# Attention and FFN block: four query projections move into attention's slots, and the softmax division moves from GpSimd to VectorE

## The chip, the cores and the metric

One core of one Trainium2 chip. The metric is the device time of one execution in microseconds (us), the median of three runs. Lower is better.

## The reference

`x` has 8 rows of 512 tokens with 256 channels. All arithmetic is fp32.

```python
xn = layernorm(x)
q, k, v = xn @ Wq, xn @ Wk, xn @ Wv            # 32 query heads, 8 key/value heads, 64 wide
q, k = rope(q), rope(k)
scores = q @ k.T / 8                           # a query sees itself and the 127 tokens before it
attn = softmax(scores)                         # per head
y1 = (attn @ v) @ Wo
h = fwht(xn * SU_ug) / 64
h = silu(h @ W_gate.T * s_gate) * (h @ W_up.T * s_up)     # 1024 wide
y2 = (fwht(h * SU_dp) / 64) @ W_down.T * s_down
out = x + y1 + y2
```

The scales `s_gate` and `s_up` are the two halves of `Wscale_ug` times 64, and `s_down` is `Wscale_dp` times 64.

## The kernel before

The kernel takes the 8 rows one after the other. Each row has two stages, the FFN and the attention. Before the first row a prologue folds the Hadamard transforms into the gate, up and down weights.

**Precision.** A projection keeps each operand as a high and a low part and multiplies them three times (`three`, lines 897 to 899): high by high, low by high, high by low. One *part* of a query projection is six matmuls with 512 columns. A query group `m` (four heads, one key/value head) has two parts. `("q", 4, 0)` in a table is group 4, `("k", 1, 0)` is the second half of the keys, and `NEXT` means that the job belongs to the next row.

**FFN stage.** PE computes gate and up for eight hidden blocks `j` into the two banks of `PROJ`. ACT applies silu (L592), VectorE multiplies (L808) and makes the low part (`h_low`, L669), and PE adds the down product two blocks later. Before the change the first hidden block of each pair from `HIDDEN_AFTER[1..3]` alternates with a part of `q1`, `q2` and `q3`.

**Attention stage.** It runs in 35 slots, `n` = 0 to 34. A step is 128 queries of one group, so a group has four steps and a row 32. In slot `n` the engines do, each in its own order:

- PE: scores of step `n` (L1041), transposes of the weights of step `n-2` (L1052, called TR(n-2) below), the *fillers* of the slot (projections, output projections `wo`, values `v`, transposes of the next row's x), and, in even slots from 4 on, the value products of steps `n-4` and `n-3` (L1071, O).
- VectorE: `fold(n)` (L823, or L828 at every fourth step) which waits for the scores, the row maxima (L830), `inverse_sum(n-1)` (L835), in odd slots the low part of O (L669, `o_low`), in the first row the splitting of weights, and then for each filler the rope products (L714) or the addition into `acc` (L741, `wo_add`).
- ACT: the copy of the transposed weights (L607), four exponentials with their sums (L597), the copy of O (L612).
- GpSimd: `normalise(n-1)` (L490), which multiplies the exponentials `e_sb` by `rinv`, `mask(n-2)` (L498), value differences (L505), and the rope rotation of a job whose second stage falls in the slot (`rotate`, L466 and L468, two operations on `prod`).

Every engine is in order, so an operation waits behind all that stands ahead of it on its engine. `fillers(b, n)` and `ROPE_SLOTS` set the slots of the projections by hand. A bank of `PROJ` is free for use `u` when use `u-2` has been read (`bank`, L917). `prod` is single, so the first product of a job waits until the rotation of the job before is done.

**SyncE's queue** copies the rotated queries and keys into `q_stack` and `k_stack` (8 and 4 small DMAs for a group), loads the split weights of `wq` and `wo` into rings of two, and stores the result. In the first row the weights come unsplit, ACT and VectorE split them at the points of `WQ_SPLIT_IN_FFN`, `WQ_SPLIT_SLOT` and `WO_SPLIT_SLOT`, and SyncE saves the split form for the later rows.

**Prologue.** The gate and up weights are folded in eight pieces of 512 columns (L763 to L780): PE multiplies by the Hadamard matrix, VectorE scales (L768), ACT takes the high part (L569), VectorE the low part (L669). PE waits for all eight (`fold_lo`, L984) before the first gate.

Of the kernel before, what the change touches and what calls it, by code (L numbers as in the profile page):

```python
# [5 lines left out]
def attention_and_ffn_block(  # L6
# [55 lines left out]
    def job(kind, n):  # L62
# [9 lines left out]
    ROPE_SLOTS = {("q", 4, 0): (3, 5), ("k", 1, 0): (7, 9), ("q", 5, 0): (11, 13),  # L72
                  ("q", 6, 0): (15, 17), ("q", 7, 0): (19, 21), ("k", 0, NEXT): (29, 31)}
    NORM_SLOT = 24

    WQ_SPLIT_IN_FFN = {1: 2, 2: 3, 3: 4}
    WQ_SPLIT_SLOT = {4: 5, 11: 6, 17: 7}
# [7 lines left out]
    def fillers(b, n):  # L85

        found = []
        if 0 < n < TT - 1:
            found.append(("v", b, 0, n + 1))
        for part in range(2):  # L90
            found += [(kind, row, m, part) for kind, m, row in rope_jobs(b, n, part)]
        if n in (STEPS + 1, STEPS + 2) and b + 1 < BATCH:
            found.append(("q", b + 1, 0, n - STEPS - 1))
# [11 lines left out]
    for b in range(BATCH):  # L105
        for n in range(4):
            for j in HIDDEN_AFTER[n]:
                if n and j == HIDDEN_AFTER[n][0]:
                    USES += [("q", b, n, 0), ("gate", b, j, 0), ("q", b, n, 1), ("up", b, j, 0)]
                else:  # L110
                    USES += [("gate", b, j, 0), ("up", b, j, 0)]
# [19 lines left out]
    with ctx:  # L131
# [65 lines left out]
        silu_sb = e_sb[:, 0, :, :].rearrange("p r q -> p (r q)")  # L197
# [102 lines left out]
        def _(sp):  # L300
# [58 lines left out]
            for b in range(BATCH):  # L359
# [33 lines left out]
                for m in (2, 3):  # L393
                    if not b:
                        save_wq(m)
                    load_wq(b, m + 2)
                if not b:
                    save_wq(4)
                for n in range(2, NKV):
# [4 lines left out]
                    if not b and n == 2:  # L404
                        save_wo(0)
                        save_wo(1)
                        save_wq(5)
                    if not b and n == 4:
                        save_wq(6)
                    if not b and n == 5:  # L410
                        save_wq(7)
                    if 3 <= n <= 4:
# [25 lines left out]
        def _(pool):  # L438
# [15 lines left out]
            def rotate(row, kind, n):  # L454

                if kind == "q" and n >= 2:

                    pool.wait_ge(*stacked(row, n - 2, q_stacked, Q_STACKED))
                if kind == "k" and (n or row):
# [25 lines left out]
            for b in range(BATCH):  # L485
                def normalise(n):
                    wait_apart(pool, "pool", rinv_done, b * STEPS + n + 1)
                    e = e_sb[:, n % 2, :, :]
                    r = rinv[:, n % 2, :].rearrange("p (r o) -> p r o", o=1).to_broadcast([P, REP, P])
                    nc.gpsimd.tensor_tensor(e, e, r, ALU.mult).then_inc(norm_done, 1)  # L490

# [16 lines left out]
                rotate(b, "q", 0)  # L508
# [4 lines left out]
                for n in range(1, 4):  # L513
                    rotate(b, "q", n)
                for n in range(STEPS + 2):
                    if 1 <= n <= STEPS:
                        normalise(n - 1)
# [648 lines left out]
```

## Time and profile before

| | |
|---|---|
| median of 3 runs | 1442.33 us (1441.26 to 1446.47) |
| the profiled execution | 1443.7 us, of which the span of the core is 1441.2 us |
| PE (TensorE) busy | 1335.5 us, 93% of the span |
| VectorE busy | 913.0 us, 63% |
| ACT busy | 745.3 us, 52% |
| GpSimd busy | 686.0 us, 48% |
| granted TensorE clock | 0.993 of full speed |

Times in the profile are counted from the start of the span. A row of the timeline gives the start and the duration of an instruction, and in brackets how long its engine sat idle before it and what it then waited for. Matmuls overlap, so the length of a run of matmuls is read from one start to the next.

### The profile page before, as it was taken

To read this page: it belongs to the slowest core of one execution; us is meant where nothing else is said; L and a number is where in the kernel's file an instruction comes from. 1 tells how busy PE (TensorE), PEld (TensorE's weight loads), DVE (VectorE), ACT (ScalarE), POOL (GpSimd) and SP (SyncE) were. 2 spreads that over 40 slices of the span, in tenths; PEclk is the share of its full clock that TensorE was granted. 3 is DMA by queue.
4 is the path that set the end of the run, shared out by engine and by line. 5 is a ranking of instruction groups with operands and counts; after the bars stand their busy time and mean duration, and the time that the engine had idled before them with its cause. 6 is when DMAs were issued, how large, how long until landed. Compare 5 with 4: busy or idle time off the path is not lost.

```text
span 1441.2 us, 34032 instructions
## 1 busy us (share of the span) xinstructions
PE 1335.5 (93%) x12776; PEld 1046.0 (73%) x12776; DVE 913.0 (63%) x1496; ACT 745.3 (52%) x2685; POOL 686.0 (48%) x719
## 2 busy tenths in 40 slices
PE   6798889989999999999989999998999999999998
PEld 3576667867777677777768777786777777777776
DVE  5656665467745677457764677556774567745775
ACT  2345564266633667146652666426663366724665
POOL 5225543266542665236542555425653266523664
PEclk9899999999999999999999999999999999999999
DMA  6223441424222342323414144042432234231331
GB/s 228 66 81 104 118 125 60 139 62 127 83 89 84 87 126 69 113 66 108 120 53 132 43 119 120 30 147 60 123 85 90 87 82 119 82 109 51 90 106 58
DMA packets 71554, 138.35 MB, mean 96 GB/s; under 512 B 15328, under 2 KB 29152, under 8 KB 71136
## 3 DMA queue, kind: packets, MB, share of 16 engines
q1 hardware_dynamic: 70400, 135.46, 32.7%
q8 instruction: 102, 1.67, 0.5%
q10 hardware_dynamic: 992, 0.73, 0.2%
q14 instruction: 60, 0.49, 0.1%
HBM read 73.21 MB, written 12.58 MB: 60 GB/s over the span
## 4 chain that ended last, share of the span: by engine, by line
PE 64%; DVE 14%; POOL 8%; issue 5%; ACT 4%; SPq 2%; DMA 1%; POOLq 0%; DVEq 0%
PE PROJ L897 14%; PE PROJ L899 13%; PE PROJ L898 13%; PE O L1071 7%; PE TR L1052 6%; POOL e_sb L490 6%; PE S L1041 5%; DVE negmax L830 3%; DVE S L828 3%; ACT e_sb L597 2%; PE S L897 2%; DVE acc L741 2%; PE S L898 2%; PE S L899 2%; DVE S L823 2%
## 5 line engine op out<-in xcount | busy, mean ns | idle before, releaser
L490 POOL TENSOR_TENSOR e_sb<-e_sb,rinv 128x512 f32<-128x512 f32 x256 | 266.2, 1040 | 354.6 <-DVE rinv L835 349.9
L597 ACT ACTIVATE e_sb<-S,negmax 128x128 f32<-128x128 f32 x1024 | 362.1, 369 | 110.3 <-DVE negmax L830 109.0
L714 DVE TENSOR_TENSOR prod<-PROJ,rope_sb 128x1024 f32<-128x1024 f32 x160 | 195.4, 1222 | 117.5 <-PE PROJ L899 116.8
L823 DVE COPY_PREDICATED S<-diagonal_key,S 128x512 f32<-128x512 int8 x192 | 133.2, 694 | 178.5 <-PE S L1041 178.3
L607 ACT ACTIVATE pt_sb<-TR 128x512 f32<-128x512 f32 x256 | 153.2, 598 | 178.8 <-PE TR L1052 176.9
L1041 PEld LDWEIGHTS S<-k_stack,q_stack 64*64 64x64 f32 x5632 | 169.6, 133 | 79.6 <-issue 53.5
L1052 PE MATMUL TR<-ident,e_sb 128*128 128x128 f32 x1024 | 168.0, 287 | 62.4 <-POOL e_sb L490 58.7
L1041 PE MATMUL S<-k_stack,q_stack 64*64 64x64 f32 (+2 forms) x5632 | 211.1, 274 | 7.8 <-ACT e_sb L597 7.8
L597 ACT ACTIVATION_READ_ACCUMULATOR e_sb<-S,negmax 128x1 f32 x1024 | 212.2, 207 | 0.0
L830 DVE TENSOR_REDUCE negmax<-S 128x4 f32<-128x512 f32 x256 | 177.0, 691 | 8.8
L1052 PEld LDWEIGHTS TR<-ident,e_sb 128*128 128x128 f32 x1024 | 108.0, 141 | 95.3 <-POOL e_sb L490 77.5
L466 POOL TENSOR_TENSOR qy<-prod 128x512 f32<-128x512 f32 x64 | 84.7, 1323 | 189.1 <-DVE prod L714 182.7
L592 ACT ACTIVATE e_sb<-PROJ 128x512 f32<-128x512 f32 x64 | 38.3, 598 | 258.9 <-PE PROJ L899 258.9
L498 POOL TENSOR_SCALAR_AFFINE_SELECT p_cur<-pt_sb 128x512 f32<-128x512 f32 x256 | 163.3, 638 | 17.4 <-ACT pt_sb L607 17.4
L897 PE MATMUL PROJ<-wo_ring,o_hi 128*128 128x256 f32 x512 | 145.4, 284 | 0.0
L898 PE MATMUL PROJ<-wo_ring,o_hi 128*128 128x256 f32 x512 | 142.9, 279 | 0.0
L899 PE MATMUL PROJ<-wo_ring,o_lo 128*128 128x256 f32 x512 | 142.9, 279 | 0.0
L1071 PE MATMUL O<-pt_sb,v_sb 128*64 128x256 f32 x768 | 120.2, 391 | 0.0
L1071 PE MATMUL O<-p_cur,v_step 128*64 128x256 f32 x768 | 116.5, 382 | 0.0
L808 DVE TENSOR_TENSOR p_cur<-PROJ,e_sb 128x512 f32<-128x512 f32 x64 | 44.3, 692 | 113.6 <-PE PROJ L899 113.6
L897 PE MATMUL PROJ<-xt_hi,wq_ring 128*128 128x512 f32 x256 | 111.8, 437 | 3.7 <-DVE prod L714 2.2
L897 PE MATMUL PROJ<-xt_hi,wgu_hi 128*128 128x512 f32 x256 | 103.1, 403 | 8.6 <-DVE wgu_lo L669 8.6
(96 smaller groups left out, 2589.4 us busy)
## 6 DMA issues: line engine op xcount, KB each, us to landing
q_stack<-qy SPq DMA_DIRECT2D x512, 64.0 KB, 2.0
wq_ring<-wq_split_d SPq DMA_DIRECT2D x56, 512.0 KB, 3.5
wo_ring<-wo_split_d SPq DMA_DIRECT2D x56, 512.0 KB, 3.9
k_stack<-ky SPq DMA_DIRECT2D x256, 64.0 KB, 2.0
x_in<-x SPq DMA_DIRECT2D x8, 512.0 KB, 4.6
wq_split_d<-wq_ring SPq DMA_DIRECT2D x8, 512.0 KB, 2.8
wo_split_d<-wo_ring SPq DMA_DIRECT2D x8, 512.0 KB, 4.0
out<-acc SPq DMA_DIRECT2D x8, 512.0 KB, 4.9
```

Source lines behind the costliest of these rows:

```text
L490: nc.gpsimd.tensor_tensor(e, e, r, ALU.mult).then_inc(norm_done, 1)
L498: nc.gpsimd.affine_select(out=p_cur[:, n % 4, :, :], in_=pt_sb[:, n % 4, :, :], compare_op=ALU.is_ge, fill=0.0, base=0, pattern=[[0, REP], ...
L597: last = nc.scalar.activation(e_sb[:, n % 2, r, :], s_heads(n, 1)[:, r, :], ACT.Exp, bias=negmax[:, n % 2, r:r + 1], accum_out=rowsum[:, n ...
L714: nc.vector.tensor_tensor(prod[:, 2 * part:2 * part + 2, :], both, rope_sb[:, :, :], ALU.mult).then_inc(prod_done, 1)
L823: nc.vector.copy_predicated(own.rearrange("p r (a k) -> p r a k", a=2), diagonal_key[:, :, :].rearrange("p r (a k) -> p r a k", a=2), diagonal
L830: nc.vector.tensor_reduce(negmax[:, n % 2, :], own, axis=AX.X, op=ALU.max, negate=True).then_inc(max_done, 1)
L897: nc.tensor.matmul(dst, lhs[0], rhs[0], start=first, stop=False)
L898: nc.tensor.matmul(dst, lhs[0], rhs[1], start=False, stop=False)
L899: return nc.tensor.matmul(dst, lhs[1], rhs[0], start=False, stop=last)
L1041: last = nc.tensor.matmul(dst[:, at:at + (blocks - 1) * step + 1:step, :], q_stack[rows, g % 2, slot, i * P + a * HP:i * P + (a + 1) * HP] ...
L1052: last = nc.tensor.transpose(TR[:, r, :], e_sb[:, n % 2, r, :], ident[:, :])
L1071: last = nc.tensor.matmul(O[odd * D:(odd + 1) * D, :].rearrange("p (m s q) -> p m s q", m=2, s=2)[:, :, n % 2, :], v[:, g * D:(g + 1) * D] ...
```

## The change

1. `q2` and `q3` leave the FFN stage and get slots 0, 1 and 4, 5 of attention. `q4` moves from slots 3, 5 to 7, 8, `k1` from 7, 9 to 10, 11, `q5`, `q6`, `q7` to 13, 14, then 17, 18, then 21, 22, the next row's `k0` from 29, 31 to 27, 28 and its `q0` from 33, 34 to 31, 32. Parts now fall in even slots too. Values 2 and 3 move from slots 1, 2 to 2, 3. The loads, saves and splits of `wq` follow, and the rotation of the next `q0` goes from the start of the row to slot 32 of the row before.
2. The multiplication of `e_sb` by `rinv` runs on VectorE right behind the reciprocal, no longer on GpSimd.
3. The folding in the prologue runs over the columns first, and each gate and up of the first row waits only for its own columns. The output of silu gets a buffer of its own instead of lying in `e_sb`.

```diff
-    ROPE_SLOTS = {("q", 4, 0): (3, 5), ("k", 1, 0): (7, 9), ("q", 5, 0): (11, 13),
-                  ("q", 6, 0): (15, 17), ("q", 7, 0): (19, 21), ("k", 0, NEXT): (29, 31)}
+    ROPE_SLOTS = {("q", 2, 0): (0, 1), ("q", 3, 0): (4, 5), ("q", 4, 0): (7, 8), ("k", 1, 0): (10, 11),
+                  ("q", 5, 0): (13, 14), ("q", 6, 0): (17, 18), ("q", 7, 0): (21, 22), ("k", 0, NEXT): (27, 28),
+                  ("q", 0, NEXT): (31, 32)}
-    WQ_SPLIT_IN_FFN = {1: 2, 2: 3, 3: 4}
-    WQ_SPLIT_SLOT = {4: 5, 11: 6, 17: 7}
+    WQ_SPLIT_IN_FFN = {1: 2, 3: 3}
+    WQ_SPLIT_SLOT = {5: 4, 9: 5, 12: 6, 18: 7}
...
-        if 0 < n < TT - 1:
-            found.append(("v", b, 0, n + 1))
+        if 2 <= n < TT:
+            found.append(("v", b, 0, n))
...
-        if n in (STEPS + 1, STEPS + 2) and b + 1 < BATCH:
-            found.append(("q", b + 1, 0, n - STEPS - 1))
...
-                if n and j == HIDDEN_AFTER[n][0]:
+                if n == 1 and j == HIDDEN_AFTER[n][0]:
...
-        silu_sb = e_sb[:, 0, :, :].rearrange("p r q -> p (r q)")
+        silu_sb = staging_rest[:, 0:T]
...
 SyncE's queue
-                for m in (2, 3):
-                    if not b:
-                        save_wq(m)
-                    load_wq(b, m + 2)
                 if not b:
-                    save_wq(4)
+                    save_wq(2)
+                load_wq(b, 4)
...
-                        save_wq(5)
-                    if not b and n == 4:
-                        save_wq(6)
-                    if not b and n == 5:
-                        save_wq(7)
-                    if 3 <= n <= 4:
+                    if not b and 2 <= n <= 6:
+                        save_wq(n + 1)
+                    if 2 <= n <= 4:
                         load_wq(b, n + 3)
...
 GpSimd
+                elif kind == "q" and row:
+                    pool.wait_ge(*stacked(row - 1, NKV + n - 2, q_stacked, Q_STACKED))
...
-                def normalise(n):
-                    wait_apart(pool, "pool", rinv_done, b * STEPS + n + 1)
-                    e = e_sb[:, n % 2, :, :]
-                    r = rinv[:, n % 2, :].rearrange("p (r o) -> p r o", o=1).to_broadcast([P, REP, P])
-                    nc.gpsimd.tensor_tensor(e, e, r, ALU.mult).then_inc(norm_done, 1)
...
-                rotate(b, "q", 0)
+                if not b:
+                    rotate(b, "q", 0)
...
-                for n in range(1, 4):
-                    rotate(b, "q", n)
+                rotate(b, "q", 1)
                 for n in range(STEPS + 2):
-                    if 1 <= n <= STEPS:
-                        normalise(n - 1)
                     if n >= 2:
                         mask(n - 2)
-                    if n in (0, 2, 3):
-                        value_step(max(n, 1))
+                    if n in (0, 3, 4):
+                        value_step(max(n - 1, 1))
...
 VectorE
-                c, k = divmod(n, 4)
+                k, c = divmod(n, CT)
...
-                def inverse_sum(n):
+                def normalise(n):
                     dve.wait_ge(exp_done, b * STEPS + n + 1)
                     nc.vector.reciprocal(rinv[:, n % 2, :], rowsum[:, n % 2, :]).then_inc(rinv_done, 1)
+                    dve.wait_ge(rinv_done, b * STEPS + n + 1)
+                    e = e_sb[:, n % 2, :, :]
+                    r = rinv[:, n % 2, :].rearrange("p (r o) -> p r o", o=1).to_broadcast([P, REP, P])
+                    nc.vector.tensor_tensor(e, e, r, ALU.mult).then_inc(norm_done, 1)
...
                 for n in range(1, 4):
-                    products(b, "q", n, 0)
-                    products(b, "q", n, 1)
+                    if n == 1:
+                        products(b, "q", n, 0)
+                        products(b, "q", n, 1)
...
 TensorE
-            pe.wait_ge(fold_lo, CT * 4)
-
...
+                    if not b:
+                        pe.wait_ge(fold_lo, CT * (j // 2 + 1))
...
-                        alternate = n and j == HIDDEN_AFTER[n][0]
+                        alternate = n == 1 and j == HIDDEN_AFTER[n][0]
```

## Rows read from the trace of the kernel before

**Rows 1.** The page, busy time: us, share of the span, instructions.
```profile
PE 1335.5 (93%) x12776; PEld 1046.0 (73%) x12776; DVE 913.0 (63%) x1496; ACT 745.3 (52%) x2685; POOL 686.0 (48%) x719
```

**Rows 2.** Windows (busy PE, PEld, DVE, ACT, POOL): one row's FFN, its attention.
```profile
584.09:633.53 49.44, 49.04 (x266) 40.96 (x264) 24.33 (x35) 13.11 (x22) 12.04 (x9) 1.00 0.37 107
633.53:755.73 122.20, 114.11 (x1329) 87.88 (x1329) 85.86 (x146) 77.83 (x310) 71.38 (x80) 1.00 0.32 88
```

**Rows 3.** Waits over the span: us in total, times, longest.
```profile
DVE wo_ring L669 <- ACT wo_ring L555: 20.7, 8, 4.0
...
PE TR L1052 <- POOL e_sb L490: 58.7, 103, 2.9
...
PE PROJ L928 <- DVE acc L741: 8.2, 7, 2.3
```

**Rows 4.** Timeline of PE: slots 12 to 17, then slot 33.
```profile
673.30 0.67 PE L1041 MATMUL S<-k_stack,q_stack 64*64 64x64 f32 x16
...
675.93 0.89 PE L1041 MATMUL S<-k_stack,q_stack 64*64 64x128 f32 x24
676.98 0.66 PE L1052 MATMUL TR<-ident,e_sb 128*128 128x128 f32 x4 [0.16 <-POOL e_sb L490]
...
680.38 0.89 PE L1041 MATMUL S<-k_stack,q_stack 64*64 64x128 f32 x24
...
683.65 0.89 PE L1041 MATMUL S<-k_stack,q_stack 64*64 64x128 f32 x24
...
691.54 0.65 PE L1052 MATMUL TR<-ident,e_sb 128*128 128x128 f32 x4 [0.16 <-POOL e_sb L490]
...
748.81 0.66 PE L1052 MATMUL TR<-ident,e_sb 128*128 128x128 f32 x4 [1.82 <-POOL e_sb L490]
```

**Rows 5.** Timeline of VectorE in slots 12 and 13.
```profile
674.13 0.75 DVE L828 COPY_PREDICATED_SCALAR S<-later_key,masked 128x512 f32 x1
...
677.01 0.70 DVE L823 COPY_PREDICATED S<-diagonal_key,S 128x512 f32<-128x512 int8 x1 [1.31 <-PE S L1041]
677.74 0.69 DVE L830 TENSOR_REDUCE negmax<-S 128x4 f32<-128x512 f32 x1
678.35 0.17 DVE L835 RECIPROCAL rinv<-rowsum 128x4 f32<-128x4 f32 x1
678.43 0.66 DVE L669 TENSOR_TENSOR o_lo<-O,o_hi 128x512 fp32r<-128x512 f32 x1
679.07 1.23 DVE L714 TENSOR_TENSOR prod<-PROJ,rope_sb 128x1024 f32<-128x1024 f32 x1
680.48 0.69 DVE L741 TENSOR_TENSOR acc<-PROJ,acc 128x512 f32<-128x512 f32 x1 [0.19 <-PE PROJ L899]
```

**Rows 6.** Timeline of GpSimd: slot 12, then slot 32.
```profile
675.88 1.04 POOL L490 TENSOR_TENSOR e_sb<-e_sb,rinv 128x512 f32<-128x512 f32 x1 [2.42 <-DVE rinv L835]
...
747.72 1.03 POOL L490 TENSOR_TENSOR e_sb<-e_sb,rinv 128x512 f32<-128x512 f32 x1
```

**Rows 7.** The operations that write `h_lo`: duration in ns, min/median/max.
```profile
L669 DVE TENSOR_TENSOR h_lo<-p_cur,h_hi x64: 681/688/1406, 52.2 to 1314.5; 128x512 fp32r<-128x512 f32 x64
```

**Rows 8.** Timeline of the FFN stage: GpSimd and VectorE near 611 us.
```profile
610.53 1.30 POOL L466 TENSOR_TENSOR qy<-prod 128x512 f32<-128x512 f32 x1 [7.07 <-DVE prod L714]
611.78 1.74 POOL L468 TENSOR_TENSOR qy<-prod 128x512 f32<-128x512 f32 x1
...
611.26 1.12 DVE L669 TENSOR_TENSOR h_lo<-p_cur,h_hi 128x512 fp32r<-128x512 f32 x1
```

**Rows 9.** Timeline of PE in the FFN stage: one part of `q2`, then a gate.
```profile
604.48 0.40 PE L897 MATMUL PROJ<-xt_hi,wq_ring 128*128 128x512 f32 x1
...
605.89 0.40 PE L897 MATMUL PROJ<-xt_hi,wgu_hi 128*128 128x512 f32 x1
```

**Rows 10.** Timeline of the prologue's end: the first gate on PE, silu on ACT.
```profile
42.94 0.79 PE L897 MATMUL PROJ<-xt_hi,wgu_hi 128*128 128x512 f32 x1 [8.56 <-DVE wgu_lo L669]
...
45.91 0.60 ACT L592 ACTIVATE e_sb<-PROJ 128x512 f32<-128x512 f32 x1 [0.98 <-PE PROJ L899]
```

More of the change, by code:

```diff
@@ L633, in _ @@
                         h_high(j - 1)
-                    if not b:
+                    if not b and n in WQ_SPLIT_IN_FFN:
                         wq_high(WQ_SPLIT_IN_FFN[n])
@@ L761, in fold_weights @@
             def fold_weights(n):
-                c, k = divmod(n, 4)
+                k, c = divmod(n, CT)
                 dve.wait_ge(fold_ready, n + 1)
@@ L774, in _ @@
             for n in range(CT * 4):
-                c, k = divmod(n, 4)
+                k, c = divmod(n, CT)
                 if n + 1 < CT * 4:
@@ L854, in _ @@
                         hidden(j)
-                    if not b:
+                    if not b and n in WQ_SPLIT_IN_FFN:
                         wq_low(WQ_SPLIT_IN_FFN[n])
@@ L868, in _ @@
                     if 1 <= n <= STEPS:
-                        inverse_sum(n - 1)
+                        normalise(n - 1)
                     if n >= 5 and n % 2:
@@ L975, in _ @@
             for n in range(CT * 4):
-                c, k = divmod(n, 4)
+                k, c = divmod(n, CT)
                 if n >= 4:
```

## The prediction

> **What bounds the kernel now.** I began with the busy times: PE works 93% of the span [rows 1], so PE's own work is the floor, and the question is where its other 7% goes. The windows of one row show it: the FFN stage leaves PE 0.40 us idle out of 49.44, the attention stage 8.1 out of 122.20 [rows 2]. VectorE is busy for 70% of attention (85.86 us), and for half of the FFN stage. The list of waits names the cause: PE waited 58.7 us for GpSimd's normalisation before its transposes, 103 times [rows 3].
>
> The timelines show a wait from inside. In slot 12 the scores end about 674.0. Fold starts at 674.13 [rows 5], GpSimd multiplies from 675.88 for 1.04 [rows 6], and TR(11) starts at 676.98, 0.16 after PE became free [rows 4]. So from fold to transposes the chain takes 2.85 us. Slots 12 to 15 repeat: TR(11) to TR(15) is 691.54 - 676.98 = 14.56 us. The long stalls lie at the ends of attention: before TR(31) PE idles 1.82 us [rows 4], because GpSimd was still rotating keys when the reciprocal was ready, and its multiplication began only at 747.72 [rows 6].
>
> **Part 1, work that changes stage.** A part of a q projection takes 605.89 - 604.48 = 1.41 us on PE [rows 9]. Four parts leave the FFN stage, with its 0.40 of idle: -6.0 us a row. The same four enter attention: +5.6, and about +0.1 for the switches between kinds of matmul: -0.3 together. The gain has to come from stalls that they fill. Each job issues the same 8 small copies on SyncE's queue as before, later by some slots; `q2` is stacked after step 3, 4 steps before its use, as it was. The new wait of the next `q0` rotation is for copies made some ten slots before: nothing.
>
> **Part 2, the multiplication on VectorE.** It takes away GpSimd's 1.04 us and the 0.18 from the end of the reciprocal (675.53 + 0.17) to GpSimd's start. It adds a 128x512 fp32 product of two SBUF operands on VectorE. No such row with `rinv` exists. The nearest is `h_lo`, also two SBUF operands and 512 columns: 0.68 to 1.41 us, median 0.69 [rows 7]. I take 0.69, with 0.61 until the next independent instruction, as from maxima to reciprocal (678.35 - 677.74) [rows 5]. The start behind the reciprocal I take as 0.20. Fold to transposes becomes 0.73 + 0.61 + 0.20 + 0.69 + 0.06 = 2.29, half a microsecond shorter, and GpSimd's rotations no longer stand ahead of it in a queue.
>
> Two things speak against it. First, VectorE gets 0.8 us more in each slot, and 18 of its 20 rope products now come in attention (14 before). For four slots with one q job and two output projections: 4 x (0.73 + 0.61 + 0.20 + 0.61) + 2 x 0.64 (`o_low`) + 2 x 1.23 + 2 x 0.69 = 13.7 us [rows 5], against PE's 14.3 without stalls. Second, `h_lo` reaches 1.41 us. Where it took 1.12 it began at 611.26 while GpSimd's two-operand subtraction ran to 611.83, and the next GpSimd operation took 1.74 and not 1.30 [rows 8]. So each waits for the other: 0.57 + 0.55 = 1.12. The new multiplication starts 1.5 us after a fold, and a rotation (two operations, 2.55 us) starts right behind the product ahead of that fold. They meet.
>
> GpSimd's mask reads one operand, and no row shows VectorE waiting for it. The Trainium skill (SBUF — State Buffer, Who interferes with whom) says that a VectorE instruction with two SBUF inputs contends with any GpSimd instruction that reads SBUF, and that the first to start holds the port to its end. For the rotations rows 8 agree. By that rule the mask blocks too, which I put at some 0.3 us a row in the sum; by the rows alone it would be zero.
>
> Now four slots by hand, from TR(11) = 0. The pieces: scores 0.81 (0.60 at every fourth step), transposes 0.41 ahead of a projection and 0.59 ahead of O, O 1.44 at the first pair of a group (675.93 - 673.30 = 2.63 = 0.60 + 0.59 + 1.44) and else 1.88 (683.65 - 680.38 = 3.27), projection 1.48 and output projection 1.50 (680.38 - 676.98 = 3.40 with the transposes) [rows 4]. Fold can start 1.07 after its scores start (0.84 at a fourth step).
> Slot 13: `q5` and output projection to 3.39; VectorE folds at -0.1, multiplies to 2.6 after a wait of 0.6 for the mask, then `o_low` 3.15, product 4.30, addition 4.92.
> Slot 14: scores 3.39; fold late at 4.92; second part of `q5` and O to 8.03; product 8.22.
> Slot 15: scores 8.03, fold 9.10; the multiplication waits from 10.64 to 10.90 for the rotation of `q5`, TR(14) 11.50; `o_low` and addition to 12.62.
> Slot 16: scores 10.83, so fold could start at 11.67 and starts at 12.62; multiplication to 14.91.
> Slot 17: scores end 14.35, TR(15) 14.95.
> So 14.95, where it was 14.56: the shorter chain is eaten by VectorE being 0.95 late behind the addition.
>
> The same by hand for the other stretches of a row gives the time that PE stands still, counted from start to start:
> - Slots 0 to 7: 3.9 now (each of the transposes 0 to 5 but one waits); after, TR(0) 0.6, TR(1) 1.6 with `q2`'s rotation in the way, TR(2) 0.15, TR(5) 1.6 with that of `q3`: 3.9.
> - Slots 8 to 23: 1.2 now; after, TR(8) 0.5, TR(11) 0.7, TR(15) and TR(19) 0.65 each: 2.5.
> - Slots 24 to 26 (next row's x): now 1.3 for the second transpose of x, which waits for the addition (8.2 us for 7 rows as idle [rows 3]), 0.75 behind it and 0.24: 2.3; after, the addition comes one multiplication later, 2.5, and TR(23) 0.6: 3.1.
> - Slots 27 to 34: now 1.8 (1.82 as idle before TR(31) [rows 4]); after, TR(28) 0.5 and 0.6 for the mask behind `q0`'s rotation: 1.1.
> Together 9.2 now and 10.6 after. A hand schedule rounds each step up a little; I take half of the difference, +0.7. A steady row comes to -0.3 + 0.7 = +0.4 us, times 7: +2.8.
>
> **Part 3, prologue, first row, last row.** The first gate waited 8.56 us for the last low part of the folded weights (`wgu_lo`) and started at 42.94. Silu on ACT was ready 0.98 before PE had its input at 45.91 [rows 10]. With two pieces the first gate and up can run before, but the second gate needs silu, and silu still stands behind ACT's part of all eight pieces: -1.0 (bounds 0 and the two parts that come early, -2.8). The first row's FFN stage loses one split of weights ahead of a projection: -1.5 (0 to -2). In its attention VectorE waited 20.7 us for ACT, to split `wo` [rows 3], with the reciprocals of later slots queued behind. The multiplication now stands ahead of that wait and uses its time: -3 (0 to -6). The last row has no next jobs; half a microsecond less chain at two stalls: -1 (0 to -3).
>
> Sum: 1441.2 + 2.8 - 1.0 - 1.5 - 3.0 - 1.0 = 1437.5 us of span. The median of the runs is 1.1 above the profiled span (1442.33), so 1438.6 us.
>
> **Rivals.**
> 1. *The multiplication seldom waits.* Against it: rows 8. For it: a product that comes 0.3 us earlier lets the rotation end sooner, and later slots have slack. Without any wait, by the same schedule, TR(1), TR(5), TR(8), TR(11) and the mask behind `q0` save 1.0, 1.1, 0.5, 0.3 and 0.6 us: 3.5 a row, 28 in 8 rows, 1411 us. With some of them 1418.
> 2. *VectorE becomes the bound* (slower). Its 13.7 us for four slots leave 0.6 below PE. If three of four multiplications wait 0.6 us, as the longest `h_lo` nearly do, it needs 13.7 + 1.8 = 15.5, 0.55 above my 14.95; over six such stretches in 8 rows +26: 1465 us. It decides as soon as the waits for GpSimd pass 1.25 us in four slots; in my schedule they are 0.9. For it: masks and rotations together take 5.1 of GpSimd's 14.6 us there, and a late fold also makes the exponentials late.
> 3. *The stages only trade.* If PE's stalls stay what they are, the moved parts are worth -0.3 a row and the time is about 1438 to 1442. This ends beside my forecast.
> 4. The change does what it says in any case: the multiplication is gone from GpSimd by construction.
>
> **How the numbers follow.** The forecast with rival 3 has 0.50 (1428 to 1450), rival 1 has 0.30 (1408 to 1430), rival 2 has 0.20 (1448 to 1475). About 0.5% is what a measurement of this kernel can tell from no change: 1435.1 to 1449.5. Faster takes rival 1 and a quarter of the forecast's spread: 0.42. Slower takes nearly all of rival 2 and a little: 0.21. The rest, 0.37, is the same. The range leaves out a tenth at either end: 1412 to 1458.
>
> **What would show it.** Right: the FFN stage near 43.4 us; the multiplication at a median near 0.70 us with a tail to 1.4 where GpSimd rotates; TR waiting for VectorE instead of GpSimd, with about 0.6 us every fourth step; VectorE at 110 us in the attention of a row; TR(31) without a wait. Wrong in part 2: a multiplication that never passes 0.75 us beside a rotation (rival 1), or fold starting late in nearly every slot (rival 2). The forecast fails most easily in slots 0 to 7 and 24 to 26, where the hand schedule has the fewest rows to lean on, and by an error of 0.5 us in one stretch that comes 8 times.

## The result and the profile after

| | before | after |
|---|---|---|
| median, on the same chip | 1442.31 us (1441.26 to 1446.47, 4 runs) | 1468.12 us (1466.95 to 1470.29, 4 runs) |
| ratio, 95% interval | | 1.0175 (1.0159 to 1.0191) |
| span of the profiled execution | 1441.2 us | 1466.8 us |
| granted TensorE clock | 0.993 | 0.986 |

The kernel became 1.75% slower. That lies above the range (1412 to 1458), on the side of rival 2.

The busy times of the page after, which answer to [rows 1]:

```profile
PE 1346.7 (92%) x12776; PEld 1053.9 (72%) x12776; DVE 1106.2 (75%) x1752; ACT 748.1 (51%) x2685; POOL 456.1 (31%) x463
```

VectorE has 256 instructions more, all of them the multiplication, and 193 us more. The groups of the page say what one costs:

```profile
L826 DVE TENSOR_TENSOR e_sb<-e_sb,rinv 128x512 f32<-128x512 f32 x256 | 228.6, 893 | 8.7
L487 POOL TENSOR_SCALAR_AFFINE_SELECT p_cur<-pt_sb 128x512 f32<-128x512 f32 x256 | 197.3, 771 | 469.2 <-ACT pt_sb L594 420.0
```

The mean of the multiplication is 893 ns. The view of the tile `e_sb` has the spread (minimum, median, maximum in ns):

```profile
L826 DVE TENSOR_TENSOR e_sb<-e_sb,rinv x256: 691/720/1764, 95.3 to 1454.7; 128x512 f32<-128x512 f32 x128
```

So 256 x (0.893 - 0.691) = 52 us of VectorE's time went into multiplications that had begun and took longer than the quickest. This sum is called the *lengthening* below. GpSimd's mask has a mean of 771 ns too, where its quickest is 625.

The windows of the row that [rows 2] show (FFN, attention), then of the first row's attention:

```profile
598.45:641.41 42.96, 42.90 (x242) 36.63 (x240) 18.74 (x31) 13.12 (x22) 3.99 (x3) 1.00 0.37 108
641.41:772.24 130.83, 120.63 (x1354) 92.55 (x1353) 115.66 (x182) 78.20 (x310) 50.27 (x53) 1.00 0.31 86
...
90.27:247.71 157.44, 129.92 (x1354) 97.16 (x1353) 122.36 (x194) 84.33 (x322) 51.10 (x53) 0.94 0.33 100
```

In the kernel before, the first attention was this window:

```profile
99.17:240.28 141.11, 119.97 (x1329) 90.69 (x1328) 91.75 (x157) 83.17 (x321) 71.67 (x80) 0.96 0.34 97
```

The attention row from 641.41 on against [rows 2]: PE's busy time grew by 120.63 - 114.11 = 6.52 us, the FFN stage shrank by 6.48, and PE's idle time in attention grew from 8.09 to 10.20. That last 2.1 us is the loss of this steady row.

The first attention is 26.6 us longer than the steady one (18.9 before), so 7.7 us of its growth are its own. The windows divide them: PE's busy time grew by 9.95 us where the steady row's grew by 6.52, and its idle time by 6.38 (from 21.14 to 27.52) where the steady row's grew by 2.11. That is 3.4 us of busy time, at a mean granted clock of 0.94 where it was 0.96, and 4.3 us of waiting.

By stages, from the starts of FFN and scores in the two timelines:

| | forecast | measured | off by |
|---|---|---|---|
| prologue and first FFN | -8.5 | -8.9 | -0.4 |
| first attention | +3.4 | +16.3 | +12.9 |
| FFN of row 1 | -6.0 | -4.4 | +1.6 |
| from the scores of row 1 to those of row 7 | +2.4 | +15.4 | +13.0 |
| last attention | +5.0 | +7.1 | +2.1 |
| span | -3.7 | +25.6 | +29.3 |

The forecasts are the terms of the prediction, put at their stage: a steady FFN -6.0, a steady attention +6.4 (5.7 for the parts and 0.7 for the stalls). Nearly half of the miss sits in one stage of one row; most of the rest is spread over all rows. The FFN of row 1 took 44.7 us, where the later ones take 42.9: PE was busy in it for 44.64 us at a granted clock of 0.96, for 42.87 at 1.00 in the next row.

**The steady loss.** The list of waits after:

```profile
PE TR L1044 <- DVE e_sb L826: 59.1, 92, 2.8
```

It takes the place of 58.7 us of waiting for GpSimd [rows 3]: the wait changed its releaser and not its size. Slots 1 and 2 show how one such wait comes about. VectorE, from a rope product on:

```profile
647.15 1.19 DVE L701 TENSOR_TENSOR prod<-PROJ,rope_sb 128x1024 f32<-128x1024 f32 x1
648.26 0.69 DVE L810 COPY_PREDICATED S<-diagonal_key,S 128x512 f32<-128x512 int8 x1
648.98 0.69 DVE L817 TENSOR_REDUCE negmax<-S 128x4 f32<-128x512 f32 x1
649.59 0.17 DVE L822 RECIPROCAL rinv<-rowsum 128x4 f32<-128x4 f32 x1
649.79 1.75 DVE L826 TENSOR_TENSOR e_sb<-e_sb,rinv 128x512 f32<-128x512 f32 x1
651.46 0.68 DVE L810 COPY_PREDICATED S<-diagonal_key,S 128x512 f32<-128x512 int8 x1
```

GpSimd over the same time, and the transposes on PE that wait:

```profile
648.49 1.27 POOL L461 TENSOR_TENSOR qy<-prod 128x512 f32<-128x512 f32 x1 [5.01 <-DVE prod L701]
649.73 1.26 POOL L463 TENSOR_TENSOR qy<-prod 128x512 f32<-128x512 f32 x1
650.95 1.09 POOL L487 TENSOR_SCALAR_AFFINE_SELECT p_cur<-pt_sb 128x512 f32<-128x512 f32 x1
```

```profile
651.60 0.66 PE L1044 MATMUL TR<-ident,e_sb 128*128 128x128 f32 x4 [1.52 <-DVE e_sb L826]
```

Read the starts. The product frees GpSimd's rotation at 648.3. Fold, maxima and reciprocal take 1.5 us, and the first rotation operation takes 1.24 to the next. So the second one starts at 649.73, 0.06 us before the multiplication, which then lasts 1.75, about the 1.2 us of the rotation and the rest of its own. In return the mask that follows takes 1.09, where it takes 0.63 alone. Both chains hang on the same product. In slot 5, behind the rotation of `q3`, they meet in nearly the same way: the rotation starts at 664.89, the multiplication at 664.96 and takes 1.75, and TR(5) waits 1.36 us.

Two of the six steady rows took 132.3 and 132.4 us of attention, the other four 130.8. PE idles the same 10.2 us in both kinds. In each of the six it waits 2.12 us for an addition at the next row's x, and in these two the granted clock fell behind that wait. Row 1, which is one of the two, then the same place in the row shown above:

```profile
292.41:424.74 132.33, 122.10 (x1353) 93.72 (x1352) 115.77 (x182) 78.20 (x310) 50.79 (x53) 0.99 0.30 86
...
391.52 1.11 PE L920 MATMUL PROJ<-ident,prod 128*128 128x128 f32 x4 [2.12 <-DVE acc L728]
392.56 1.56 PE L1033 MATMUL S<-k_stack,q_stack 64*64 64x128 f32 x24
...
740.55 0.66 PE L920 MATMUL PROJ<-ident,prod 128*128 128x128 f32 x4 [2.12 <-DVE acc L728]
741.13 0.89 PE L1033 MATMUL S<-k_stack,q_stack 64*64 64x128 f32 x24
```

PE's busy time is 122.10 us against 120.63, so the 1.5 us are clock. Why it fell behind two of six equal waits the traces don't show.

**The first row.** Late in the first attention VectorE's order puts the low part of the weights ahead of the next row's x:

```profile
196.57 0.69 DVE L826 TENSOR_TENSOR e_sb<-e_sb,rinv 128x512 f32<-128x512 f32 x1
200.90 0.69 DVE L656 TENSOR_TENSOR wo_ring<-wo_stage,wo_ring 128x512 fp32r<-128x512 f32 x1 [3.63 <-ACT wo_ring L542]
201.51 1.38 DVE L684 TENSOR_SCALAR prod<-x_in,moments,rstd 128x256 f32<-128x256 f32 x4
```

```profile
202.06 1.21 PE L920 MATMUL PROJ<-ident,prod 128*128 128x128 f32 x4 [2.67 <-DVE prod L684]
206.28 1.11 PE L920 MATMUL PROJ<-ident,prod 128*128 128x128 f32 x4 [3.01 <-DVE acc L728]
207.32 1.56 PE L1033 MATMUL S<-k_stack,q_stack 64*64 64x128 f32 x24
```

VectorE stands still for 3.63 us until ACT has the high part, and all that PE needs next is queued behind it. PE idles 2.67 and 3.01 us, and the windows show the clock at that time:

```profile
200.00:205.00 5.00, 1.21 (x4) 0.55 (x4) 4.03 (x10) 2.32 (x8) 0.45 (x1) 0.88 0.45 105
205.00:210.00 5.00, 3.73 (x34) 2.94 (x36) 3.40 (x7) 1.42 (x7) 0.51 (x1) 0.50 0.42 140
```

After a stretch in which PE was busy for 1.21 of 5 us the granted clock is 0.50, the 1.2 GHz level, and the scores take 1.56 us instead of 0.88.

### The profile page after: what moved, and what is told of

Same layout as the page of the kernel before. It is cut to its first block and busy times, and to the rows that moved or that the text cites. A ratio compares the mean times of both kernels' runs of the same rounds, so it can differ in the third digit from the quotient of the medians.

```text
span 1466.8 us, 33805 instructions
## 1 busy us (share of the span) xinstructions
PE 1346.7 (92%) x12776; PEld 1053.9 (72%) x12776; DVE 1106.2 (75%) x1752; ACT 748.1 (51%) x2685; POOL 456.1 (31%) x463
## 3 DMA queue, kind: packets, MB, share of 16 engines
q8 instruction: 103, 1.69, 0.5%
## 5 line engine op out<-in xcount | busy, mean ns | idle before, releaser
L487 POOL TENSOR_SCALAR_AFFINE_SELECT p_cur<-pt_sb 128x512 f32<-128x512 f32 x256 | 197.3, 771 | 469.2 <-ACT pt_sb L594 420.0
L826 DVE TENSOR_TENSOR e_sb<-e_sb,rinv 128x512 f32<-128x512 f32 x256 | 228.6, 893 | 8.7
L1044 PE MATMUL TR<-ident,e_sb 128*128 128x128 f32 x1024 | 169.4, 289 | 63.9 <-DVE e_sb L826 59.1
L1033 PE MATMUL S<-k_stack,q_stack 64*64 64x64 f32 (+2 forms) x5632 | 214.6, 276 | 0.0
L810 DVE COPY_PREDICATED S<-diagonal_key,S 128x512 f32<-128x512 int8 x192 | 132.4, 689 | 60.0 <-PE S L1033 58.6
L795 DVE TENSOR_TENSOR p_cur<-PROJ,staging_rest 128x512 f32<-128x512 f32 x64 | 44.3, 692 | 171.3 <-PE PROJ L891 170.6
L889 PE MATMUL PROJ<-wo_ring,o_hi 128*128 128x256 f32 x512 | 148.2, 290 | 0.0
L579 ACT ACTIVATE staging_rest<-PROJ 128x512 f32<-128x512 f32 x64 | 38.3, 598 | 208.3 <-PE PROJ L891 208.2
L890 PE MATMUL PROJ<-wo_ring,o_hi 128*128 128x256 f32 x512 | 143.1, 280 | 0.0
L599 ACT ACTIVATE o_hi<-O 128x512 fp32r<-128x512 f32 x128 | 77.1, 602 | 69.2 <-PE O L1063 69.2
```

The costliest lines, as they stand in the source:

```text
L487: nc.gpsimd.affine_select(out=p_cur[:, n % 4, :, :], in_=pt_sb[:, n % 4, :, :], compare_op=ALU.is_ge, fill=0.0, base=0, pattern=[[0, REP], ...
L826: nc.vector.tensor_tensor(e, e, r, ALU.mult).then_inc(norm_done, 1)
L889: nc.tensor.matmul(dst, lhs[0], rhs[0], start=first, stop=False)
L890: nc.tensor.matmul(dst, lhs[0], rhs[1], start=False, stop=False)
L1033: last = nc.tensor.matmul(dst[:, at:at + (blocks - 1) * step + 1:step, :], q_stack[rows, g % 2, slot, i * P + a * HP:i * P + (a + 1) * HP] ...
L1044: last = nc.tensor.transpose(TR[:, r, :], e_sb[:, n % 2, r, :], ident[:, :])
```

## The experiments

The ratio of each is against the kernel before on the same chip (medians 1443.52, 1443.38 and 1443.53 us in three sets; the table above has 1442.31). Differences between kernels of two sets are between medians, and hold to about 1 us.

### Each part alone

`moves_only` has parts 1 and 3, the new slots and the new fold order, with the multiplication back on GpSimd ahead of the mask (the new slots without the new fold order did not run):

```diff
 GpSimd
+                    if 1 <= n <= STEPS:
+                        normalise(n - 1)
                     if n >= 2:
                         mask(n - 2)
 VectorE, normalise(n)
-                    dve.wait_ge(rinv_done, b * STEPS + n + 1)
...
-                    nc.vector.tensor_tensor(e, e, r, ALU.mult).then_inc(norm_done, 1)
```

> The changed kernel with one part undone: GpSimd multiplies again, behind the reciprocal, as before the change; the new slots and the new folding stay. Theory A (VectorE's multiplication meets GpSimd's rotations and queues ahead of the folds, and that costs the 25 us): near or below the kernel before, 1430 to 1445 us. Theory B (the new slots are the loss, whoever multiplies: a rotation behind a product in an even slot stands ahead of the next multiplication on GpSimd as well): 1455 us or more, and transposes 1 and 5 wait for GpSimd over 1 us each.

`mult_only` is the kernel before with the multiplication on VectorE: the same lines the other way round.

> The kernel before with one part of the change alone: the multiplication on VectorE behind the reciprocal; slots, folding and all else as before. Theory A: slower than before, 1450 us or more, since each multiplication adds 0.6 us to VectorE ahead of the next fold. Theory B: VectorE has four products fewer in attention here, the chain from fold to transposes is half a microsecond shorter and the 1.8 us wait at each row's end goes: 1428 to 1438 us.

`fold_only` is the kernel before with part 3:

```diff
-                c, k = divmod(n, 4)
+                k, c = divmod(n, CT)
...
-            pe.wait_ge(fold_lo, CT * 4)
+                    if not b:
+                        pe.wait_ge(fold_lo, CT * (j // 2 + 1))
```

> The kernel before with the third part alone: the folding over the columns first, the silu buffer of its own. All theories: the first gate starts near 36 us, the FFN of the first row ends 1 us earlier, 1441 us (0 to 2.8 us less than before). If it is slower than before, the clock after the gap on PE is why.

| | us | ratio | row: FFN / attention | first attention |
|---|---|---|---|---|
| moves_only | 1435.29 | 0.9953 (0.9936 to 0.9969) | 42.94 / 126.8 | 152.9 |
| mult_only | 1438.94 | 0.9976 (0.9961 to 0.9991) | 49.1 / 121.7 | 143.1 |
| fold_only | 1442.86 | 0.9995 (0.9986 to 1.0004) | | |

None of these makes the kernel slower. Parts 1 and 3 give -8.2 us, part 2 -4.6 and part 3 -0.7 (-0.5%, -0.2% and nothing), all together +1.75%. The same multiplication that gains 4.6 us in the old slots costs 32.8 in the new ones, so the loss is an interaction of part 2 with the other two, and as part 3 alone does nothing, most likely with part 1. `moves_only` did what its first theory said. `mult_only` fell between its two, 0.9 us above the range of the second.

The number of meetings with GpSimd does not tell the two kernels apart: the lengthening is 44.0 us in `mult_only` and 51.7 in the changed kernel. What differs is where PE waits. TR waits 42.0 us for VectorE in `mult_only` and 59.1 in the changed kernel; in a steady row PE idles 7.6 and 10.2 us. In the changed kernel 2.9 us of that row's idle time are the waits of TR(1) and TR(5), behind the rotations of `q2` and `q3`, which `mult_only` does in the FFN stage.

The first attention is longer than a steady one by 18.9 us before, by 21.4 in `mult_only`, 26.1 in `moves_only` and 26.6 in the changed kernel. So what the first row loses of its own comes mostly with the new slots, whoever multiplies.

In `fold_only` the first gate starts at 35.55 us instead of 42.94, and yet the scores of the first row start at 99.26 instead of 99.17: what PE begins earlier it waits for again, so part 3's prologue is worth nothing.

### GpSimd's operations out of the way

`rot_late` keeps all the work and lets GpSimd rotate one slot later, behind the next multiplication and its mask:

```diff
-                    for kind, m, row in rope_jobs(b, n, 1):
-                        rotate(row, kind, m)
+                    for kind, m, row in rope_jobs(b, n - 1, 1):
+                        pool.wait_ge(norm_done, b * STEPS + min(n, STEPS))
+                        rotate(row, kind, m)
```

> The changed kernel, but GpSimd starts a rotation only when the multiplication of the next slot is done, so the two never meet. Theory A1 (the meeting is what costs): multiplications stay below 0.9 us, transposes 1 and 5 lose waits of 1.5 and 1.4 us, the same in the first row: 25 us less, near 1443 us. Theory A2 (the load of VectorE is what costs, the meetings hide in it): 0 to 8 us less than the changed kernel, 1460 to 1468 us.

`rot_memset` is the changed kernel with both rotation operations replaced by memsets of the same tiles, so the rotation is left out; `all_memset` replaces the masks too, so rotation and masking are left out.

```diff
-                nc.gpsimd.tensor_tensor(y[:, 0, :], prod[:, 0, :], prod[:, 3, :], ALU.subtract
-                                        ).then_inc(rotated, 1)
+                nc.gpsimd.memset(y[:, 0, :], 0.0).then_inc(rotated, 1)
...
 all_memset also
-                    nc.gpsimd.affine_select(out=p_cur[:, n % 4, :, :], in_=pt_sb[:, n % 4, :, :], compare_op=ALU.is_ge,
...
+                    nc.gpsimd.memset(p_cur[:, n % 4, :, :], 0.0).then_inc(p_masked, 1)
```

> The changed kernel with both operations of every rotation replaced by a memset of the same destination on GpSimd, so they read nothing and are shorter; the rotated queries and keys are zeros, the rotation is left out. VectorE's work and all slots stay as in the changed kernel. Theory A (meeting the rotations costs 20 us of the 25): no multiplication over 1.0 us, 1440 to 1448 us. Theory C (the meetings hide, what the late rotation saved was something else, such as the place of the masks): 1460 us or more.

> As the run before, and the masks are memsets too (the masking is left out), so in attention GpSimd reads SBUF only for three value differences a row. If the masks meet the multiplication as well, the multiplication's median falls from 0.72 to 0.69 us and the time by another 1 to 8 us against the run before; if they do not, both are equal within 1 us. What is left over the kernel with the new slots and GpSimd's multiplication (1435.3) is then VectorE's queue alone: 0 to 8 us.

`rot_late` ran in 1446.73 us, ratio 1.0023 (1.0014 to 1.0033), 21.4 us below the changed kernel, where its first theory said near 1443. But its premise did not hold. The multiplication and a steady row of `rot_late`:

```profile
L827 DVE TENSOR_TENSOR e_sb<-e_sb,rinv x256: 691/834/1712, 96.7 to 1430.1; 128x512 f32<-128x512 f32 x128
...
628.33:756.66 128.33, 120.85 (x1354) 92.46 (x1353) 115.80 (x182) 78.04 (x310) 48.40 (x53) 1.00 0.31 87
```

The maximum is still 1712 ns where 0.9 us was expected, the median rose from 720 to 834, and the lengthening is 51.0 us, as in the changed kernel. The meetings moved to other places: TR(1) waits 0.46 us instead of 1.52, TR(5) 0.30 instead of 1.36, and PE idles 7.5 us in the row instead of 10.2. So this run shows that what a meeting costs depends on whether PE waits for that multiplication.

`rot_memset` ran in 1436.16, 0.9945 (0.9930 to 0.9960), and `all_memset` in 1424.53, 0.9864 (0.9849 to 0.9878). The multiplication in `rot_memset`, then in `all_memset`:

```profile
L824 DVE TENSOR_TENSOR e_sb<-e_sb,rinv x256: 691/693/1170, 94.5 to 1421.4; 128x512 f32<-128x512 f32 x128
```

```profile
L822 DVE TENSOR_TENSOR e_sb<-e_sb,rinv x256: 691/691/1694, 94.2 to 1410.7; 128x512 f32<-128x512 f32 x128
```

Each multiplication can be sorted by the GpSimd operation that was running when it began (lengths in us):

| | nothing: count, longest | rotation: count, median | mask: count, median, longest | lengthening, us |
|---|---|---|---|---|
| changed kernel | 115, 0.694 | 42, 1.47 | 91, 0.84, 1.17 | 51.7 |
| mult_only | 113, 0.695 | 47, 1.17 | 88, 0.84, 1.17 | 44.0 |
| rot_late | 92, 0.694 | 22, 1.69 | 134, 0.84, 1.17 | 51.0 |
| rot_memset | 136, 0.694 | | 112, 0.83, 1.17 | 18.8 |
| all_memset | 143, 0.694 | | 104 (memsets), 0.69, 0.694 | 3.0 |

The 8 or 9 that are missing in each line began during a value difference. So a multiplication is lengthened only where it begins under a GpSimd operation that reads SBUF, the mask with its one operand included, and a memset in the mask's place lengthens none of 104. In `all_memset` the 9 that pass 0.7 us, the 1694 ns among them, are those that began during a value difference.

In time, the rotations are worth 32.0 us and the masks another 11.6: 43.6 of 1468.1. Both lie outside what was expected (1440 to 1448 us, then 1 to 8 less), and `all_memset` ends 10.8 us below `moves_only`, where 0 to 8 above was expected. These are upper values for the meetings alone, since memsets also free GpSimd earlier and PE waits for the masks too. The Trainium skill (SBUF — State Buffer, Who interferes with whom) has GpSimd's reads behind the port that a VectorE instruction with two SBUF inputs needs, and by it the mask, with one operand, must block too. The trace of the changed kernel agrees for both: medians of 1.47 us behind a rotation and 0.84 behind a mask, where 0.69 is the undisturbed length.

### The order on VectorE

A theory of its own was that the multiplication is late because fold stands ahead of it. `norm_first_rot_late` is `rot_late` with the two exchanged:

```diff
+                    if 1 <= n <= STEPS:
+                        normalise(n - 1)
                     if n < STEPS:
                         fold(n)
-                    if 1 <= n <= STEPS:
-                        normalise(n - 1)
```

> The kernel with the late rotation (1446.7 us), and VectorE multiplies at the start of a slot, ahead of the fold, where it otherwise sits idle until the scores are there. Theory E (the place in VectorE's queue costs the rest): transposes hardly wait for VectorE (below 15 us in all, 41.8 now), 1425 to 1436 us. Theory F (VectorE's total load is what is left, wherever the multiplication stands): 1443 to 1450 us. If the exponentials come too late for it, the fold is late in every slot and it is slower, 1455 us.

It ran in 1531.51 us, 1.0624 (1.0585 to 1.0663), 85 us above `rot_late`. The waits say why:

```profile
ACT e_sb L585 <- DVE negmax L818: 435.3, 256, 3.7
...
DVE rinv L823 <- ACT e_sb L585: 142.1, 178, 1.6
```

VectorE now waits for the exponentials of step n-1 before it folds step n, and ACT waits for the maxima before each of the 256 steps. Each stands idle for the other in turn. With the fold ahead of the multiplication ACT gets its maxima in time. The expectation had named this case and put it at 1455 us, 77 too low. What the place behind the fold costs by itself this run can't say, since the new wait covers it.

`by_head_split` tests another escape, an instruction with one SBUF tensor. It has the later splitting of the next section as well, and four multiplications of 128 columns with the scalar from `rinv`:

```diff
-                    nc.vector.tensor_tensor(e, e, r, ALU.mult).then_inc(norm_done, 1)
+                    for r in range(REP):
+                        e = e_sb[:, n % 2, r, :]
+                        last = nc.vector.tensor_scalar(e, e, rinv[:, n % 2, r:r + 1], None, ALU.mult)
+                    last.then_inc(norm_done, 1)
```

> The changed kernel with the low parts one slot later, and VectorE multiplies in four instructions of 128x128, each with its head's 1/sum as a scalar by pointer, so each has one tensor input from SBUF. Theory G (only the second tensor input meets GpSimd): none takes over 0.35 us, 1415 to 1430 us. Theory H (this form meets GpSimd as well, or four starts cost more than one long instruction): single ones over 1 us beside rotations, 1440 us or more.

It ran in 1511.89 us, 1.0479 (1.0462 to 1.0497), 64 us above `split_late`, from which it differs in this alone. VectorE and GpSimd in its steady row:

```profile
693.15 1.63 DVE L826 TENSOR_SCALAR e_sb<-e_sb,rinv 128x128 f32<-128x128 f32 x4
...
701.26 0.88 DVE L826 TENSOR_SCALAR e_sb<-e_sb,rinv 128x128 f32<-128x128 f32 x4
```

```profile
692.46 1.27 POOL L463 TENSOR_TENSOR ky<-prod 128x512 f32<-128x512 f32 x1
```

Undisturbed, the four take 0.88 us where one took 0.69. Beside a rotation they take 1.63: the rotation ends at 693.73, 0.58 us after they begin. So one tensor operand doesn't escape, as the second theory had it. The Trainium skill (VectorE: DVE Perf Modes, Mode 2×_2P) says that such an operation may read one SBUF tensor through both ports; the 1.63 fits that, and no run here separates it from another cause. Attention became 137.9 to 140.7 us a row, 7 to 10 more than in `split_late`. In the row from 640.70 to 781.28 VectorE is busy for 126.0 us, 10.3 more than in the changed kernel's row, of which 6.1 are the 0.19 us more in each of 32 slots. What VectorE got in addition the row lost nearly in full, so VectorE sets much of the pace here; part of it is clock, 0.96 in that row.

### The splitting of weights in the first row

`split_late` is the changed kernel in which VectorE makes the low parts of `wq` and `wo` one slot after ACT makes the high parts:

```diff
-                    if not b and n in WQ_SPLIT_SLOT:
-                        wq_low(WQ_SPLIT_SLOT[n])
+                    if not b and n - 1 in WQ_SPLIT_SLOT:
+                        wq_low(WQ_SPLIT_SLOT[n - 1])
...
 and the same for wo
```

> The changed kernel with VectorE's low parts of the first row's weights one slot later, as in the run that took the kernel with GpSimd's multiplication from 1435.3 to 1413.0 us. If the first row's loss is a thing of its own, the gain adds: 1446 us, the first attention near 136 us where it was 157.4. If the multiplication on VectorE fills that wait, as the prediction had it, the gain is small: above 1455 us.

The same edit was made to `rot_late` (`rot_split`), to `moves_only` (`moves_split`) and to the kernel before (`before_split`).

> The changed kernel with both: rotations behind the multiplication, low parts one slot later. If the two gains are separate: 1446.7 less some 18 to 22 us, 1425 to 1429 us; masks still meet the multiplication, so it stays above 1413.

> The new slots with GpSimd's multiplication (1435.3 us), and in the first row VectorE makes the low part of a weight one slot after ACT made the high part, not in the same slot. Theory D (VectorE's wait for ACT in even slots is what makes the first row's attention 152.9 us long where a steady one takes 126.8): VectorE's wait for ACT at wo_ring falls from 24 us to below 3, the first attention to 135 to 143 us, the time to 1418 to 1427. If the first row is long for its loads and saves, nothing changes.

> The kernel before, with nothing of the change, and the low parts one slot later. It waited 20.7 us for ACT there and its first attention is 141.1 us where a steady one takes 122.2. Expected 1428 to 1436 us, the first attention 128 to 134 us. Then the new slots with GpSimd's multiplication are worth the difference to 1413.

| | us | ratio | without the later split | first attention |
|---|---|---|---|---|
| split_late | 1447.79 | 1.0030 (1.0019 to 1.0040) | 1468.12 | 137.2 (157.4) |
| rot_split | 1429.84 | 0.9905 (0.9890 to 0.9920) | 1446.73 | 135.7 (149.7) |
| moves_split | 1413.04 | 0.9785 (0.9770 to 0.9799) | 1435.29 | 132.0 (152.9) |
| before_split | 1431.14 | 0.9915 (0.9899 to 0.9931) | 1443.53 | 129.1 (141.1) |

The first attention of `split_late`, to be held against the 157.44 row above:

```profile
90.66:227.84 137.18, 122.92 (x1354) 93.75 (x1353) 123.31 (x194) 83.76 (x322) 51.51 (x53) 0.99 0.37 109
```

The clock is back at 0.99, PE's busy time falls by 7.0 us and its idle time by 13.3, from 27.5 to 14.3. Steady attention stays at 130.84. The wait for ACT is gone: `moves_only` and then `moves_split` in the list of waits.

```profile
DVE wo_ring L664 <- ACT wo_ring L550: 24.1, 7, 4.8
```

```profile
DVE wo_ring L664 <- ACT wo_ring L550: 1.3, 3, 0.6
```

So the first-row wait was worth 12.4 us in the kernel before and 16.9 to 22.3 in the three kernels with the new slots. `split_late` and `before_split` came as expected; `rot_split` ended 0.8 us above its range and `moves_split` 5 us below its own. `moves_split` is the best of all: 2.15% below the kernel before. Its steady attention:

```profile
434.76:561.68 126.92, 119.92 (x1353) 91.63 (x1353) 90.02 (x150) 78.58 (x310) 78.32 (x85) 1.00 0.32 89
```

Against the changed kernel's row VectorE has 25.6 us less, GpSimd 28 more, and PE idles 7.0 us instead of 10.2. With the first row mended, the new slots with the new fold order are worth 1413.0 - 1431.1 = -18 us, and the multiplication on VectorE costs 1447.8 - 1413.0 = +35.

Not tried was `rinv` in PSUM, which would take one of the two SBUF operands away.

## Why the prediction was wrong, step by step

- **The bound.** Right that PE is the floor and that VectorE is the danger. VectorE is at 115.66 us of attention (said 110).
- **Part 1, the FFN stage**: said 43.4, measured 42.96. In `moves_only` PE's busy time falls by 6.16 us in FFN and grows by 5.88 in attention (said 5.7): -0.28, the trade of -0.3 as forecast. There the row is 169.8 us against 171.7, because the parts also fill stalls of PE, which idles 6.65 us in attention instead of 8.09; this gain the forecast had not credited. In the changed kernel attention grows by 6.52 of busy time and the trade is worth nothing. Where the further 0.64 comes from stays open.
- **Part 2, the multiplication**: 0.69 alone was right (minimum 691 ns), the blocking was right, and so were most of the places: TR(1) 1.52 (said 1.6) and TR(5) 1.36 (1.6), about 0.6 every fourth step (0.27 and 0.37 in two halves), x 2.1 (2.5), nothing at TR(31). From TR(11) to TR(15) the row takes 15.25 us, where the hand schedule had 14.95 and rival 2 15.5. The tail went to 1.76 and not to 1.41.
- **Part 2, the failed step of the steady row,** is a size: "I take half of the difference, +0.7". By hand the row had 9.2 us of stalls before and 10.6 after. Measured are 8.1 and 10.2 us of idle time, +2.1: the schedule after was nearly right, the one before was 1.1 too high, and the halving made the difference smaller instead of larger. With the 0.3 of the trade this makes 1.7 us a row, 10 of the 13.0 in the table. The other 3 are the two rows in which the clock fell, 1.5 us each; no term stood for that. The mask, put at 0.3 us a row, is worth up to 11.6 / 8 = 1.45 by the runs; it is a part of the idle time and does not come on top.
- **Part 3, the first row**, failed in its sign and made almost half of the miss. Two steps failed. One is "the multiplication now stands ahead of that wait and uses its time: -3". The wait did shrink, from 20.7 us [rows 3] to 14.6, and in `mult_only`, with the old slots, to 13.3. But the time did not come back: against its steady row the first attention grew by 2.5 us there. The other is that the new slots had no term of their own in the first row. In `moves_only`, where GpSimd multiplies, the first attention exceeds a steady one by 26.1 us and not 18.9. The low parts of `wo` stay in their slots, but slots 28 and 32 now also hold a product and slot 12 two splits, and what waits behind a split stops PE. The first attention grew by 16.3 us instead of 3.4. Of the 12.9 between them 2.2 are the steady row's miss, 3.0 the credit that never came, and 7.7 the first row's own growth, 3.4 of it busy time at the lower clock and 4.3 waiting. `split_late` takes 20.3 off by moving nothing but the split. The FFN of row 1 behind it lost another 1.6 us to the clock.
- **The prologue**: -1.0 forecast, nothing measured (`fold_only`), inside its bounds. So it is partly luck that prologue and first FFN together came to -8.9, where -8.5 was forecast.
- **Last row**: -1.0 forecast (FFN -6.0, attention +5.0), measured -6.1 + 7.1 = +1.0. Its stalls were not followed one by one.
- **The rivals.** Rival 2 named the mechanism (each multiplication that waits makes the next fold late) and 1465 us; that this is near 1468 is partly chance. Its 26 us were to fall in six equal stretches of every row. Some 15 us fell in the steady rows, and it had no word of the first row's splits. Rival 1 is refuted by the 127 of 256 multiplications that took more than 0.74 us. Rival 3, that PE's stalls stay what they are, fell too: they went down in `moves_only` and up in the changed kernel.

## What to carry over

Before an elementwise operation moves from GpSimd to VectorE, line up the start times of the two engines' SBUF operations over a few slots, and mark the meetings that the bounding engine waits for. `rot_late` has as much lengthening as the changed kernel and is 21.4 us faster. Two chains that hang on one product meet in nearly the same way in each row. When one engine makes the high part and another the low part of a split, let the second do it a slot later, since the wait hits what is queued behind it. Price the first row by itself when work changes its slots. Run the parts of a change alone and together: here what ran alone was neutral or better and the sum was 1.75% worse.

## What the hardware showed that was not expected

- A VectorE multiplication that starts 0.06 us behind a GpSimd operation takes 1.75 us instead of 0.69, and the GpSimd mask behind it 1.09 instead of 0.63. I had taken 1.41 as the most.
- A GpSimd mask with one SBUF operand slows it as well: behind a mask the median is 0.84 us and the longest 1.17. None of the 104 multiplications that began during a memset passed 0.694 us.
- Idle stretches of PE of 2.67 and 3.01 us in the first row went with a granted clock of 0.50 in the 5 us that hold the second. Waits of 2.12 us at the same place of six steady rows were followed by the lower clock in two and not in the other four; each fall cost about 1.5 us.
